# Own-row products of a graph layer, moved from that layer into the attention layer before it

## The reference

```
h = relu(layernorm(x)); x = x + attention(h, adj)                                    # layer 0, 4 heads
h = relu(layernorm(x)); x = x + h @ W_self + (adj @ h / max(deg, 1)) @ W_neigh       # layer 1, "the second layer"
h = relu(layernorm(x)); x = x + gru(relu(adj @ h @ W_msg.T + b_msg), h)              # layer 2
h = relu(layernorm(x)); x = x + hyperbolic(h, adj)                                   # layer 3
```

## Time and profile before

| | |
|---|---|
| median of 3 runs | 611.81 us |
| the profiled execution, its own time | 611.1 us |
| its span in the trace | 609.3 us |
| PE busy | 567.1 us, 93% of the span |
| attention's row tiles on PE | 33.6 to 176.1 us of the span |
| layer 1 on PE | 176.1 to about 305 us |

### The profile page before, as it was taken

The page is one execution under the profiler, slowest core; times in us unless marked ns, Lnnn a source line. Parts: engine busy times, 40 slices in busy tenths (PEclk is TensorE's granted clock), DMA queues, the critical chain, the costliest instruction groups (busy, mean ns, idle before and its releaser), DMA issues.

```text
span 609.3 us, 12243 instructions
## 1 busy us (share of the span) xinstructions
PE 567.1 (93%) x4599; PEld 357.0 (59%) x4599; DVE 339.2 (56%) x1483; ACT 219.6 (36%) x588; POOL 100.2 (16%) x104
## 2 busy tenths in 40 slices
PE   5679899999999899999999999999999999999981
PEld 4478899999864445545544545555554444555541
DVE  5882472233333543333314587797779853576786
ACT  5530000000001211111133587778778665432433
POOL 4770100000000100000000111111112210320311
PEclk9979999999999999999999999999999999999996
DMA  8999999999910000000000000000000011111000
GB/s 232 108 108 108 107 109 109 109 108 108 108 19 4 1 1 0 1 1 1 0 1 0 1 19 18 1 18 19 17 2 19 18 43 45 35 51 38 18 35 34
DMA packets 13655, 27.05 MB, mean 44 GB/s; under 512 B 1056, under 2 KB 1696, under 8 KB 13600
## 3 DMA queue, kind: packets, MB, share of 16 engines
q0 software_dynamic: 8704, 16.78, 27.4%
q1 hardware_dynamic: 4896, 9.51, 4.6%
HBM read 72.43 MB, written 4.19 MB: 126 GB/s over the span
## 4 chain that ended last, share of the span: by engine, by line
PE 82%; DVE 10%; issue 3%; POOL 1%; ACT 1%; DMA 1%; another core or an unknown queue 0%; SPq 0%; DVEq 0%; POOLq 0%; ACTq 0%
PE acc L1505 50%; PE acc L1324 9%; PE acc L1325 9%; PE acc L1351 4%; PE acc L1358 3%; PE acc L1344 2%; PE acc L1403 1%; PE acc L1402 1%; PE acc L1401 1%; DMA x<-x_rows 1%; POOL rs L983 1%; PE acc L1437 1%; PE acc L1408 1%; POOL region_st L983 1%; PE acc L1299 1%
## 5 line engine op out<-in xcount | busy, mean ns | idle before, releaser
L1505 PE MATMUL acc<-adj,hs_a 128*128 128x512 fp8e4 x1024 | 229.7, 379 | 2.3 <-DVE hs_a L525 1.6
L1505 PEld LDWEIGHTS acc<-adj,hs_a 128*128 128x128 f16 x1024 | 98.8, 98 | 113.3 <-DVE hs_a L525 1.8
L1324 PE MATMUL acc<-region_op,adj 128*128 128x133 f16 x1024 | 127.1, 224 | 7.2 <-issue 3.6
L1325 PE MATMUL acc<-region_op,adj 128*128 128x132 f16 x1024 | 127.0, 224 | 0.0
L1505 PE MATMUL acc<-adj,region_op 128*128 128x512 fp8e4 x512 | 118.7, 379 | 0.0
L1324 PEld LDWEIGHTS acc<-region_op,adj 128*128 128x128 fp8e4 x1024 | 101.1, 99 | 9.6 <-issue 3.7
L1325 PEld LDWEIGHTS acc<-region_op,adj 128*128 128x128 fp8e4 x1024 | 101.2, 99 | 0.1
L1505 PEld LDWEIGHTS acc<-adj,region_op 128*128 128x128 f16 x512 | 49.2, 98 | 56.3 <-issue 4.0
L983 POOL TENSOR_TENSOR region_st<-region_st,small 128x4 f32<-128x4 f32 (+1 forms) x39 | 44.9, 1152 | 207.0 <-ACT w L1118 133.9
L983 POOL TENSOR_TENSOR rs<-rs,small 128x4 f32 (+3 forms) x27 | 31.0, 1148 | 275.1 <-DVE rs L362 257.1
L1100 ACT ACTIVATE hs_a<-rowbuf 128x512 f32 x8 | 5.0, 630 | 137.0 <-DVE rowbuf L368 137.0
(11 more groups left out here) (238 smaller groups left out, 700.9 us busy)
## 6 DMA issues: line engine op xcount, KB each, us to landing
adj<-adj_pieces POOLq DMA_DIRECT2D x32, 512.0 KB, 65.3
p_rows<-rowbuf SPq DMA_DIRECT2D x8, 256.0 KB, 2.0
region_op<-p_rows SPq DMA_DIRECT2D x8, 256.0 KB, 3.1
out_rows<-x SPq DMA_DIRECT2D x7, 256.0 KB, 2.0
x<-x_rows SPq DMA_DIRECT2D x3, 512.0 KB, 7.1
region_st<-matrices SPq DMA_DIRECT2D x1, 768.0 KB, 9.3
x<-x_rows SPq DMA_DIRECT2D x2, 256.0 KB, 4.2
out_rows<-x SPq DMA_DIRECT2D x2, 128.0 KB, 1.7
```

Source lines behind the costliest of these rows:

```text
L1324: mm(bank[TG + it % TG][:, 0:HI], adj8[:, it, jt, :], op0[:, jt, 0:HI], start=(jt == 0), stop=False)
L1325: last = mm(bank[TG + it % TG][:, 0:LO], adj8[:, it, jt, :], op0[:, jt, HI:OPW], start=False, stop=(jt == NT - 1))
L1505: last = mm(dst, hs[:, jt, part, :], adj8[:, c * TG:(c + 1) * TG, jt, :], start=(k == 0), stop=(k == 2 * NT - 1))
```

## The change

- **TensorE.** `own_transposes` of groups 0 to 5 now stand in the attention, in front of row tiles 10, 14, ..., 30, and `own_self` of these groups in front of row tiles 11, 15, ..., 31 (group = tile // 4 - 2). Their result goes to bank 3, which the attention doesn't use. Groups 6 and 7 keep the places that groups 0 and 1 had in aggregates 1 and 2, and bank 4. No own-row step is left at k = 50 and 60.
- **VectorE.** The instruction that adds the own product becomes `add_own`. For groups 0 to 5 it stands in the attention, between `low_operand` and the wait for the group's four tiles, and signals `self_read`. In layer 1 groups 0 and 1 are written out one after the other, with an `add_own` for groups 6 and 7; groups 2 to 7 are a loop without one.
- **ScalarE.** Its copies of groups 0 to 5 move into its attention loop, in front of `high_part`; its layer-1 groups 0 and 1 are written out, and the rest is a loop without a copy.
- **Waits.** `own_self(0)` waits for `w16_ready`; the later ones wait until bank 3 or 4 was read (`self_read`) instead of for `xnew_ready`. `neighbours(s)` takes over the wait for `xnew_ready`.
- The alternative form gets its own copy of the moved steps, which is jumped over as before. Nine semaphores that nothing used are no longer declared.

```
             def attend(g, prev, own=None):
...
                 if prev is not None:
                     low_operand(prev, 0, xn, hs_a)
+                if own is not None:
+                    add_own(own, bank[3])
                 dve.wait_ge(S["acc_full"], (g + 1) * TG)
...
+            def add_own(g, src):
+                dve.wait_ge(S["l1_self"], g + 1)
+                rows = x[:, group_of(g), :]
+                v.scalar_tensor_tensor(rows, tiles(src), w_unsplit[:, M_SELF:M_SELF + 1], rows, ALU.mult,
+                                       ALU.add).then_inc(S["self_read"], 1)
...
-                me.link(v.scalar_tensor_tensor(x[:, group_of(g), :], tiles(bank[4]), w_unsplit[:, M_SELF:M_SELF + 1],
-                                               x[:, group_of(g), :], ALU.mult, ALU.add))
+                if isinstance(g, int):
+                    add_own(OWN_EARLY + g, bank[4])
...
+            layer1(0)
+            layer1(1)
+            with dve.Fori(2, NG) as g:
+                me.loop(g - 2, TG + 2 * TG + 1 + (TG - 1))
+                layer1(g)
...
+            with act.Fori(2, NG) as g:
+                own_rows_T(g - 2, 0)
+                high_part(g, 0, xn, hs_a, ACT.Relu)
...
-            own = {1: {50: own_transposes, 60: own_self}, 2: {43: own_transposes}, 3: {}}
+            own = {1: {}, 2: {43: own_transposes}, 3: {}}
...
+                if it >= 2 * TG and it % TG == 2:
+                    own_transposes(it // TG - 2)
+                if it >= 2 * TG and it % TG == 3:
+                    own_self(it // TG - 2)
                 tile_is_in(it)
                 attend(it, range(NT)).then_inc(S["acc_full"], 1)
```

More of the change, by code:

```diff
@@ L59 @@
 TURN_END = TURN_OPERAND + TURNS_OPERAND * NT
+TURN_OWN = TURN_END + 1
+TURNS_OWN = 4
+OWN_EARLY = NG - 2
 MASKED = 1e9
@@ L228, in build_graph_stack @@
             "top_ready", "topall_ready", "w16_ready", "odd_ready", "odd_sum", "flag_ready", "turn", "gen_in",
[L229 removed]
+            "pre_tr", "pre_hT", "sum_ready", "agg_full", "aThi_ready", "aT_ready", "l1_self", "self_read", "l1_neigh",
             "msg_full", "msg_ready", "gates_full", "rz_ready", "t_ready", "n_ready", "u_ready", "uT_full",
@@ L485, in spread_is_wide, with attend @@
                 me.link(v.tensor_tensor(wide, wide, rden[:, 4:5], ALU.max))
-            def attend(g, prev):
+            def add_own(g, src):
[3 more added lines that the diff above has]
+                                       ALU.add).then_inc(S["self_read"], 1)
+            def attend(g, prev, own=None):
                 last = isinstance(g, int) and g == NG - 1
@@ L559, in _ @@
                 me.loop(g - 2, 4 + 2 * TG + 1 + TG - 1)
-                attend(g, g - 1)
+                attend(g, g - 1, g - 2)
             me.end(NG - 3)
-            attend(NG - 1, NG - 2)
+            attend(NG - 1, NG - 2, NG - 3)
             def general_attention():
@@ L650, in general_attention @@
                 prepare_weights(Steps(dve, S["gen_step"]))
+                with dve.Fori(0, OWN_EARLY) as g:
+                    dve.wait_ge(turn, g * TURNS_OWN + (TURN_OWN + 3))
+                    rows = x[:, group_of(g), :]
+                    v.scalar_tensor_tensor(rows, tiles(bank[3]), w_unsplit[:, M_SELF:M_SELF + 1], rows, ALU.mult,
+                                           ALU.add).then_inc(turn, 1)
             dve.wait_ge(S["odd_sum"], 1)
@@ L669, in low_aggregate, with layer1 @@
                                        ALU.subtract).then_inc(S["aT_ready"], 1)
-            with dve.Fori(0, NG) as g:
-                me.loop(g, TG + 1 + 2 * TG + 1 + (TG - 1))
+            def layer1(g):
                 low_aggregate(g, 0)
-                dve.wait_ge(S["l1_self"], g + 1)
                 dve.wait_ge(S["l1_neigh"], g + 1)
@@ L685, in _ @@
                 low_operand(g, NG, tiles(dT), hs_b)
-            me.end(NG)
+            layer1(0)
[3 more added lines that the diff above has]
+                layer1(g)
+            me.end(NG - 2)
             C = col4
@@ L1138, in _ @@
                         a.activation(logits, logits, ACT.Exp, bias=gmax, accum_out=gden).then_inc(S["turn"], 1)
-                act.wait_ge(S["turn"], TURN_END + 1)
+                with act.Fori(0, OWN_EARLY) as g:
+                    act.wait_ge(S["turn"], g * TURNS_OWN + (TURN_OWN + 1))
+                    a.activation(hT16, tr16, ACT.Copy).then_inc(S["turn"], 1)
+                act.wait_ge(S["turn"], TURN_OWN + TURNS_OWN * OWN_EARLY)
                 act.wait_ge(S["w16_ready"], 2)
-            with act.Fori(0, NG) as g:
-                own_rows_T(g, 0)
+            for g in range(2):
+                own_rows_T(OWN_EARLY + g, 0)
+                high_aggregate(g, 0, False)
+                high_part(g, NG, tiles(dT), hs_b, ACT.Relu)
+            with act.Fori(2, NG) as g:
                 high_aggregate(g, 0, False)
@@ L1345, in split_transposes, with own_row @@
                 return last
+            def own_row(t, part):
+                return hs_a[:, t, part, :].rearrange("p a d -> p (a d)")
             def rows_times(srcT, m, dst):
@@ L1370, in own_self, with neighbours @@
                 if s:
+                    pe.wait_ge(S["self_read"], s)
+                else:
+                    pe.wait_ge(S["w16_ready"], 1)
+                if s >= OWN_EARLY:
+                    pe.wait_ge(S["acc_read"], NG)
+                rows_times(hT16, M_SELF, bank[3] if s < OWN_EARLY else bank[4]).then_inc(S["l1_self"], 1)
+            def neighbours(s):
+                pe.wait_ge(S["aT_ready"], s + 1)
+                if s:
                     pe.wait_ge(S["xnew_ready"], s + NG)
                 else:
[L1373 to L1377, removed]
+                    pe.wait_ge(S["flag_ready"], 1)
                 rows_times(aT16, M_NEIGH, bank[3]).then_inc(S["l1_neigh"], 1)
@@ L1491, in aggregate @@
                     if s == 1 and k in both_zero:
-                        both_zero[k](0)
+                        both_zero[k](0 if both_zero[k] is neighbours else OWN_EARLY)
                     if s == 2 and k in both_one:
-                        both_one[k](1)
+                        both_one[k](1 if both_one[k] is neighbours else OWN_EARLY + 1)
                     if k and s not in (0, 1, 2) and s <= FIRST and k in after[(s - 1) // NG + 1]:
@@ L1563, in _ @@
                 pe.wait_ge(S["w16_ready"], 2)
+                with pe.Fori(0, OWN_EARLY) as g:
+                    pe.wait_ge(turn, g * TURNS_OWN + TURN_OWN)
+                    split_transposes(lambda part, t: own_row(tile_of(g, t), part)).then_inc(turn, 1)
+                    pe.wait_ge(turn, g * TURNS_OWN + (TURN_OWN + 2))
+                    rows_times(hT16, M_SELF, bank[3]).then_inc(turn, 1)
                 aggregate(0, 0, 56)
```

16 lines of the change are left out of this document (8 added, 8 removed).

## The result

The changed kernel takes 604.75 us, the median of 4 runs (603.32 to 606.67), against 611.88 of the kernel before in the same session: ratio 0.9876 [0.9853, 0.9899], a gain of 6.2 to 9.0 us. The forecast was 607.9 with a range of 606.6 to 610.1.

A forecast was written before the change was run, and what follows sets the result against it. TensorE, busy 93% of the span, was taken as the bound. Filled transfer waits (-2.94) and group 2's shorter wait in layer 1 (-0.97) sum to -3.91 us: 607.9 against the median of 611.81, range 606.6 to 610.1.

The forecast's parts named there:

- Groups of tiles from tile 8 on take 17.17 + 1.12: Attention: each group grows only by its moved transposes and products, to 18.29 us, in the last two groups as well.
- (a): Attention: each of the twelve visits loses 0.18 us beside its instructions; -1.75 in all, 610.1 us; chance 0.13.
- Of 2.30 lost, 1.33 come back: Layer 1, group 2: 2.30 us of loss goes, a new 1.33 wait for VectorE's operand appears; gain 0.97.
- The entry: VectorE in layer 1, entering the loop behind group 1: taken at 0.77 us, as at the attention's loop.
- shorter code: VectorE in layer 1: group 1 without register steps could give a few tenths of a us more; left out.
- The lower bound of the wait, 0.56: Layer 1, group 2's neighbours' products: without any loop entry, ScalarE's high part still leaves a 0.56 us wait.
- The 2.94 us come back: Attention's last two groups: moved work fills TensorE's waits for adjacency transfers, so 2.94 of 6.72 us cost nothing.
- The sum of -4.63 by that rule: Total if VectorE's loop entry costs 0.05 us: new wait 0.61, layer-1 gain 1.69; the prediction kept -3.91.
- (b): Layer 1: loop entry takes 1.74 us or more, only the transfers' part stays; -2.94, 608.9 us; chance 0.12.
- (c): Layer 1: VectorE's loop entry costs nothing, the wait at its lower bound; -4.68, 607.1 us; chance 0.07.
- (e): Attention: later row tiles make transfers land later too, the 2.94 not won; -0.97, 610.8 us; chance 0.03.
- (d): TensorE behind the jump: second code load, 4.1 us, and fallen clock, 2.2; +2.4, 614.2 us; chance 0.05.

The follow-up runs named there:

- the run with two loops: Changed kernel with VectorE's written-out layer-1 groups 0 and 1 made a loop of two turns; 606.27 us, ratio 0.989.
- the kernel with 24 transfers: Kernel before with only 24 of 32 adjacency transfers issued, later tiles reading data of the tiles eight before; 607.53 us, ratio 0.9933.
- one experiment: Kernel before with 8 useless transposes and 12 useless products at the same twelve places, nothing moved; 620.1 us, ratio 1.0138.
- the kernel without group 2's step: Kernel before with group 2's own transposes, products and copy left out, ScalarE's groups 0 to 2 written out; 609.36 us, ratio 0.9951.
- late-start run: Kernel before with three idle powers on GpSimdE ahead of its first 1/deviation, meant to delay the attention's start; 612.59 us, ratio 1.0001.

## Why the prediction was wrong in size

- "The waits for transfers are gone": right. "Groups of tiles from tile 8 on take 17.17 + 1.12": right to 0.01, so a visit costs its instructions and (a) is out. The margin of the first products was 0.57, as forecast (0.41 by their start).
- "Of 2.30 lost, 1.33 come back": the first term that was mis-sized, and the one that every profile shows. A new wait of 1.33 was forecast and 0.30 measured, a gain of 2.00 instead of 0.97. The entry was 0.43 (0.77 taken), and shorter code, which was named, called "a few tenths" and left out of the sum, was worth 0.76 here (0.70 against the run with two loops, whose chain takes 8.69). The lower bound of the wait, 0.56, rested on the time of ScalarE's relu in the loop's form and so fell too. The step that failed here was to put the shorter code at nothing: 0.7 to 0.8 us in a chain of which each step counted in full.
- "The 2.94 us come back": the second. 2.96 came back in the two executions compared, as forecast, but 3.9 to 4.3 by the means of three each (4.1 [2.8, 5.4] by the kernel with 24 transfers). The step that failed here was to take the hole from one execution and carry its sum over to the median. The transfers' clock starts at T0 and TensorE's at S, and in that execution S was the latest of three (60.77 after T0). The holes are larger where S is earlier, and the kernel before doesn't show an early S in its time, so its median told nothing of it.
- Together the two terms explain 2.1 to 2.5 of the 3.2 us between 607.9 and 604.75. The rest is open.
- Rule and row on the loop's entry: entries and turns of VectorE's loop took 0.43 to 0.77 in the rows of four kernels. All of them are far above the 0.05 that the Trainium skill (Advanced Engine Details and Errata, Control Flow Timing) gives for a branch that is always taken. The sum of -4.63 by that rule came nearer because group 1's chain was 0.76 shorter, not because the entry cost 0.05.
- (b) is out, since the entry took 0.43 and not 1.74. (c) is out as a mechanism, since the entry cost something, though the wait fell below its 0.56. (e) is out: no wait for a transfer is left, and E moved with S. (d) did not happen here, but its like happened in one experiment.
- From group 3 on, 14.67 and no other change: right, 5.6 in all six executions.

## What to carry to other kernels

Where a stage ends with waits for transfers, its hole is the difference of two clocks: compare the distances from the first issue and from the first dependent instruction over several executions before a sum is made from one. Work put into such a hole costs nothing up to the transfers' end, and afterwards the stage's end follows the scatter that the hole had hidden. Where a wait hangs on a short chain of small instructions, count the loop's steps between them as well; here they were worth 0.8 us of 8.75.

## What the runs showed of the chip

TensorE's granted clock fell behind some single waits. In the run with two loops the wait ahead of the first aggregate was 2.47 us, and the aggregates behind it took 2.66 instead of 1.90:

```profile
69.52 2.66 PE L1547 MATMUL acc<-adj,hs_a 128*128 128x512 fp8e4 x8 [2.47 <-DVE hs_a L537]
```

```profile
70.00:76.00 6.00, 6.00 (x59) 4.72 (x58) 4.19 (x21) 0.19 (x1) 1.02 (x1) 0.72 1.06 107
76.00:90.00 14.00, 14.00 (x230) 13.72 (x228) 8.16 (x35) 1.46 (x2) 0.00 (x0) 1.00 1.06 109
```

The clock's column is the third from the end: 0.72 as the mean of 6 us, then the full level of 2.4 GHz again. This run of the changed form pays for it, since nothing behind it takes it up: from 69.52 to its aggregate after the last tile, at 181.01, are 111.49 us, 1.6 more than the 109.87 of the others. In the kernel before the hole hides the same loss. Waits of 2.08 and 2.89 us in this place (the second execution of before, and the kernel without group 2's step) had 0.72 in the same stretch; waits of 0.20 to 1.62 in nine others kept 1.00. The wait for ScalarE's copy stands on both sides: it was 1.94 to 2.04 us in six profiles, and the clock stayed at 1.00 behind it in five, the three executions of before among them. In the late-start run it fell:

```profile
214.24 1.25 PE L1355 MATMUL acc<-region_st,hT 128*128 128x128 f16 x12 [1.95 <-ACT hT L1111]
215.29 4.06 PE L1509 MATMUL acc<-adj,hs_a 128*128 128x512 fp8e4 x12
```

```profile
214.00:219.00 5.00, 4.76 (x24) 2.52 (x25) 0.85 (x2) 0.78 (x2) 0.00 (x0) 0.66 0.00 0
```

12 aggregates took 4.06 us instead of 2.75, so this execution paid some 1.3 more for that wait. The changed kernel has no such wait there, and that may be part of its gain; seen in one of the six profiles that have this wait, its share is open. Open too is why S varies by 3 us (in the six profiles of the two kernels GpSimdE is idle for 12.9 to 15.2 us ahead of the 1/deviation that releases it, for nothing that the profile shows), and why the median of the first four runs lies below the sum.
